# A fused decoder layer on one core: VectorE adds the cross-attention residual before it normalises x1

## The reference

```
x = layernorm(x + attn(x))          # gated linear recurrence over the tokens; gives x1
x = layernorm(x + xattn(x, ctx))    # cross attention, 16 heads of 16, softmax; gives x2
x = layernorm(x + ffn(x))           # 256 -> 768 -> 256, gated, quantised weights and activations
```

## Time and profile before

| | us |
|---|---|
| median of 3 timed runs | 2299.24 |
| lowest and highest | 2298.08, 2299.51 |
| the profiled execution, its own time | 2293.58 |
| its span | 2291.9 |
| busy: PE, DVE, ACT, POOL | 2122.2, 1663.3, 1145.6, 311.0 |

### The profile page before, as it was taken

How to read it: one execution, slowest core, us unless ns; L and a number is a source line. 1 busy time by engine, 2 the same in 40 slices (tenths; PEclk the granted TensorE clock), 3 DMA queues, 4 the chain that set the end, 5 groups by cost and what they waited for, 6 DMA issues and landing times. The chain is left out here.

```text
span 2291.9 us, 74706 instructions
## 1 busy us (share of the span) xinstructions
PE 2122.2 (93%) x30263; PEld 1440.3 (63%) x30263; DVE 1663.3 (73%) x3010; ACT 1145.6 (50%) x1887; POOL 311.0 (14%) x282
## 2 busy tenths in 40 slices
PE   6989998989989869999999999999899999999698
PEld 4666666666666657777777777776444444444487
DVE  7777776777777757677776767775555558989897
ACT  3444443444444436766667676665211118855365
POOL 5000000000000011111111111111000005445221
PEclk9999999999999979999999999999899999999899
DMA  3010010010000010101101010100000004459674
GB/s 107 21 30 22 25 27 21 23 29 21 26 26 21 21 47 30 42 27 34 35 27 41 27 41 27 41 27 1 1 0 0 0 1 192 192 211 424 233 269 163
DMA packets 78311, 146.48 MB, mean 64 GB/s; under 512 B 10035, under 2 KB 63542, under 8 KB 78134
## 3 DMA queue, kind: packets, MB, share of 16 engines
q1 hardware_dynamic: 78134, 143.70, 17.9%
HBM read 82.84 MB, written 60.82 MB: 63 GB/s over the span
## 5 line engine op out<-in xcount | busy, mean ns | idle before, releaser
L1281 PE MATMUL ff_bank<-ff_xq,w_uh 128*128 (+1 forms) x1536 | 457.8, 380 | 2.8 <-ACT ff_whole L1390 2.8
L1281 PE MATMUL ff_bank<-ff_xq,w_ul 128*128 (+1 forms) x768 | 291.5, 380 | 0.0
L1281 PEld LDWEIGHTS ff_bank<-ff_xq,w_uh 128*128 128x128 f16 x1536 | 149.9, 98 | 181.3 <-issue 4.1
L1595 DVE TENSOR_REDUCE ff_top<-ff_bank 128x512 f32 (+1 forms) x192 | 132.7, 691 | 116.7 <-PE ff_bank L1281 116.7
L465 ACT ACTIVATE x<-rec_e 128x512 f32<-128x512 f32 x192 | 112.0, 596 | 176.9 <-PE rec_e L348 176.9
L1390 ACT ACTIVATE ff_whole<-ff_bank,ff_coef 128x512 int16<-128x512 f32 x192 | 124.5, 682 | 103.5 <-PE ff_bank L1281 46.4
L1062 DVE TENSOR_REDUCE mneg<-att_s 128x4 f32<-128x512 f32 x256 | 158.9, 683 | 21.1 <-PE att_s L819 20.3
L600 DVE TENSOR_TENSOR rec_tmp<-rec_x,x 32x256 f32<-32x256 f32 (+1 forms) x192 | 80.8, 421 | 126.9 <-PE rec_x L385 62.1
L564 DVE TENSOR_TENSOR x<-rec_x,rec_until 128x512 f32<-128x512 f32 x256 | 158.4, 679 | 12.8 <-PE rec_x L332 12.0
L360 PE MATMUL rec_x<-x 32*32 32x64 f32 x8192 | 147.9, 218 | 21.3 <-issue 12.0
L360 PEld LDWEIGHTS rec_x<-x 32*32 32x32 f32 x8192 | 124.6, 106 | 59.3 <-issue 58.8
(11 more groups left out here) (236 smaller groups left out, 4406.9 us busy)
## 6 DMA issues: line engine op xcount, KB each, us to landing
gate_scratch<-ff_out SPq DMA_DIRECT2D x28, 768.0 KB, 3.5
ff_in<-gate_scratch SPq DMA_DIRECT2D x28, 768.0 KB, 11.0
product_scratch<-ff_out SPq DMA_DIRECT2D x28, 768.0 KB, 9.7
ff_out<-product_scratch SPq DMA_DIRECT2D x28, 768.0 KB, 5.9
att_x<-in_x SPq DMA_DIRECT2D x32, 256.0 KB, 2.7
att_ctx<-in_ctx SPq DMA_DIRECT2D x32, 256.0 KB, 2.9
att_o<-rec_scratch SPq DMA_DIRECT2D x32, 256.0 KB, 3.7
out<-s_out SPq DMA_DIRECT2D x16, 512.0 KB, 3.3
```

What stands on the lines that cost most here:

```text
L1281: m = T.matmul(bank_[:], weights(wp, kc, a, c), tile[:, xp, kc], start=(i == 0), stop=(i == len(terms) - 1))
L1595: V.tensor_reduce(top[:, k, bass.ds(n, 1)], banks[k % 6][:], AX.X, ALU.max, apply_absolute_value=True).then_inc(q1["maxed"], 1)
```

## The change

In VectorE's step the call of `residual` for the first batch moves from behind `apply` of x1 to in front of it and of the waits that belong to it. Nothing is added or removed. In the first step (no attention yet) and in the last two (no front) the order stays as it was, so 31 steps change.

```diff
                     if front:
                         dve.wait_ge(q["res1_ready"], p + 1)
                         stats(res1, st_1, mv_1, q["var_1"], q["c_stats_1"], p)
+                    if attn:
+                        residual(n0, so, 0, p - 1)
+                    if front:
                         wait_if(dve, q["x1b_ready"], p)
                         apply(res1, mv_1, rs_1, q["rstd_1"], x1, q["x1_ready"], p)
                     if attn:
-                        residual(n0, so, 0, p - 1)
                         stats2(n0, 0)
                         apply2(n0, 0)
```

## The result

The changed kernel takes 2289.52 us in the median of 20 runs, the kernel before 2295.18 in 20 runs beside them: ratio 0.9976, 95% interval 0.9966 to 0.9986. By the ratio that is 5.5 us faster (7.8 to 3.2). The forecast was 6.4 us faster and 2292.8 us, with a range down to 2290.0.

What follows compares the result with a forecast made beforehand. The attention stage, set by TensorE's loop (23.48 us a step) with the load's loop close behind, was taken as the bound. 27 steps gaining 0.26 us, with small corrections, gave -6.4 us: 2292.8 us from 2299.24, range 2290.0 to 2299.3.

Steps and rivals of the forecast that it cites:

- the stall that goes: TensorE's gap before the second batch's `values` matmuls (L849), waiting for the residual to free the PSUM bank: 14.6 us.
- Loop A: TensorE's closed loop from `values` through keys, scores and exponentials to `values` again: 23.48 us a step before, 23.17 predicted.
- The allowance for the first query: First query matmul may lose a little waiting for ScalarE's copy of x1's transpose: 0.5 us allowed in all.
- The terms put at nothing for POOL's x1b and the root for x2: Both move 0.19 us later behind x1; claimed to cost nothing, as VectorE needs nothing of them before att_attT.
- Loop B: Closed loop from x1 through SyncE's load of att_o and VectorE to the next x1: typically 22.99 us, 23.18 predicted.
- The delay of x1: On VectorE, x1 starts behind the residual, so it and SyncE's loads come 0.19 us later.
- The residual's lag: Time from the end of TensorE's output projection (L864) to the residual's start on VectorE: 0.03 us, from the epilogue.
- the two long steps: Two steps already long because of a late load; each was to get longer by 0.19 us, +0.4 together.
- The sum: 27 steps gaining 0.26 us each (7.0 us), less small costs in the other steps and the first query: -6.4 us.
- Rival 1: SyncE's load takes nearly all the gain, with x1 delayed by 0.43 us: -0.8 us, 2298.4 us; chance 0.27.
- rival 2: `values` does not come forward, because it waits for the exponentials and not the bank: 2299.2 us; chance 0.05.
- rival 3: Slower: late landings of SyncE's loads become more common; 15 such steps would give 2306 us; chance 0.08.

## Why the prediction was right or wrong

**What bounds the kernel, and the stall that goes: right.** `values` waited for the residual, now for the exponentials, at 0.05 to 0.06 behind their end.

**Loop A, 23.17 us: right.** The kernel with early loads runs at 23.17 in every step but the first and the last. The allowance for the first query (0.5 us in all, loop A up to 23.20) was not needed: the new wait for ScalarE's x1T stands in the waits (4.4 us there too), but the keys' wait right behind it takes it all back. The terms put at nothing for POOL's x1b and the root for x2 hold too: VectorE's x2 waits for its root 34.5 us in this kernel and 22.6 before (874 to 1554 us), and the step is 23.17 all the same.

**Loop B and its room, 0.41 us at a wait of 0.92 and 0.49 at the typical one: right**, tested at two delays on either side of the room. Its steps in the changed kernel follow it: one of the longer ones has its moments at +6.22 from the root's end, and the next root 23.43 later; late landings cost their full excess, the early steps of 23.80 and 23.65 are again two of the first four. The same check over all ten profiles, 28 steps of each (the first two and the last left out): the step from root to root is the longer of loop A (23.48 or 23.49 before, 23.17 changed) and the moments' start from the root's end + 17.21, within 0.06 us in every one of them. By this rule loop B is the longer in 2 of 28 steps before, in 16 of 28 in either profile of the changed kernel, in all 28 with the loads 1.36 us later and in none with the loads early.

**The delay of x1, 0.19 us: nearly.** Measured from the root's end, x1 went from 0.10 to 0.30 to 0.35, thus by 0.20 to 0.25. The residual's lag (0.04) and the 0.34 between starts are as the rows said: x1 starts before the residual's 0.42 us are over. For a later start the prediction had quoted the section "The DRAIN you can't avoid" of "VectorE: DVE Perf Modes" in the Trainium skill. That section goes on to say that a next instruction which is not held starts earlier, and this trace agrees with that second half; the prediction had used the first half only. The other 0.05 comes with loop B: in the steps that the load paces, TensorE's L864 ends 0.03 ahead of the root's end instead of 0.08, and the residual behind it is as much later. It is so in the two long steps of the kernel before and in all with the loads 1.36 us later, and in none with the loads early. So in the steps where the delay counts it is 0.25 and not 0.19.

**The sum, -6.4 us: right.** The timed ratio gives -5.5 (7.8 to 3.2), the stage in the profiles -6.9 to -8.2. Its terms are each off by less than 1 us, and the errors partly cancel. The steps without the two long ones take 23.25 us and not 23.22; the 0.5 for the first query is not there; and the 0.19 more that each of the two long steps was to take can't be seen (23.80 and 23.65 against 23.92 and 23.77 in the first profiles, 23.69 and 23.56 against 23.55 and 23.82 in the second), since their landings scatter by more. Rival 1 (the load takes nearly all) was on the right resource, with a delay that is not there; rival 2 is refuted by the releaser and the start of L849; rival 3 needed late landings to become common, and there are again two of them.

**The absolute time: wrong, and with it the range.** The step that failed is "the same 6.4 off the median 2299.24 gives 2292.8". Three runs within 1.4 us of each other looked like a kernel that repeats to 0.06%. In 20 runs its median is 2295.18, and its times spread from 2287.2 to 2299.9; in the later comparisons from 2282.3 to 2304.4. The base was 4.1 us too high. The profiled execution had stood at 2293.58, 5.7 below the median shown. I wrote that down with a forecast of 2287.2 for it, and let the range go by the other base alone. It was already the sign that executions differ by as much as the change brings. (The changed kernel's profiled execution took 2290.99: its attention stage is 6.9 us shorter, but began 4.3 us later.) And the range held only the doubts about the change (its lower end was loop A alone, 9.2 us off that base), with nothing for the base's own scatter: some 4 us more on either side would have been due (an estimate: single runs of the 20 scatter by 3.2 us, one standard deviation, thus a median of three by some 2, and twice that is taken).

What moves the base is placed, but its cause is not shown. In ten profiles the attention stage begins between 826.1 and 839.8 us. The granted clock of the first 820 us was 0.97 in the first profile of before and 0.96 in the second, and 1.00 from 880 to 1540 us in both:

```profile
0.00:820.00 820.00, 725.40 (x17216) 511.35 (x17216) 609.23 (x914) 328.67 (x577) 37.50 (x38) 0.97 0.11 29
880.00:1540.00 660.00, 643.48 (x8140) 490.53 (x8142) 471.20 (x1264) 448.70 (x817) 106.53 (x141) 1.00 0.11 34
```

```profile
0.00:820.00 820.00, 732.02 (x17216) 514.85 (x17216) 606.94 (x912) 329.19 (x577) 37.25 (x38) 0.96 0.11 29
880.00:1540.00 660.00, 643.44 (x8139) 490.61 (x8132) 471.71 (x1263) 449.40 (x816) 105.85 (x140) 1.00 0.11 34
```

(Columns: window, length, busy us of PE, PEld, DVE, ACT and POOL, clock, DMA share, GB/s.) TensorE is busy 6.6 us longer for the same 17216 matmuls in the second, and the stage begins 3.4 us later. But the changed kernel's first profile has 0.97 as well and begins at 838.7, so at this resolution the clock does not order the profiles.

The timed runs tell more, as each has the mean granted clock of its whole execution, to 0.001. Of the kernel before, 35 executions timed beside four of the experiments have clocks from 0.967 to 0.976. The 11 at 0.970 and below have a median of 2295.2 us, the 11 at 0.974 and above one of 2289.4. In the 23 executions timed beside the other four it is 2297.6 (5 of them) against 2289.3 (11), and in the changed kernel's 20 it is 2293.9 (6) against 2285.7 (4). So slower executions are those with the lower clock, by 6 to 8 us over these few thousandths, as much as the change brings. That the clock is the cause, and what lowers it, no run here shows; and it leaves a scatter of some us at equal clock.

## What to carry to other kernels

When a stall goes, look for the next closed loop through every queue that the moved instruction now stands in front of, SyncE's included, and measure each loop in a step where it decides: a wait that costs nothing (26 us for the load) can be half a microsecond a step from setting the pace. If two loops come out equal, test the pair of edits, not each alone. And take the base of an absolute forecast from the scatter of whole executions, with the profiled one counted among them; a stage's length in the profile tells a small edit's effect far more sharply than the span.

## What the runs showed of the hardware

The attention stage repeats to within 0.1 us (765.8 and 765.8) to 0.8 us (769.7 and 768.9) from execution to execution at a granted clock of 1.00, while the recurrence ahead of it, with the same code, varies over 13.7 us in ten profiles. I had expected no such difference between stages. What follows the attention stage takes one of two lengths, 678.2 to 678.7 us in six profiles and 680.6 to 680.9 in four, with no order by kernel; why is open. The loads that land latest (0.3 to 0.9 us behind the usual) come in the first four steps of the loop in both kernels' profiles, and with the loads delayed as well; with the early release they are hidden and no longer seen.
